# The second attention of a decoder kernel: two heads at a time on the two halves of the array's rows

## The reference

```python
qkv = x @ W_qkv + b_qkv
qkv = qkv.reshape(B, N, 3, NUM_HEADS, HEAD_DIM)
qkv = jnp.transpose(qkv, (2, 0, 3, 1, 4))
q, k, v = (qkv[0], qkv[1], qkv[2])
scores = jnp.einsum('bhqd,bhkd->bhqk', q, k) * SCALE
attn = jax.nn.softmax(scores, axis=-1)
out = jnp.einsum('bhqk,bhkd->bhqd', attn, v)
out = jnp.transpose(out, (0, 2, 1, 3)).reshape(B, N, C)
return out @ W_proj + b_proj
```

## Time and profile before

| | us |
|---|---|
| median of three runs | 2764.35 |
| profiled execution | 2767.74 |
| its span | 2765.9 |
| TensorE busy | 2511.4 (91%) |
| TensorE weight loads | 1727.1 (62%) |
| VectorE busy | 1717.4 (62%) |
| ScalarE busy | 1282.2 (46%) |
| GpSimd busy | 867.3 (31%) |

### The profile page before, as it was taken

The page is one execution under the profiler, slowest core; times in us unless marked ns, Lnnn a source line. Parts: engine busy times, 40 slices in busy tenths (PEclk is TensorE's granted clock), DMA queues, the critical chain, the costliest instruction groups (busy, mean ns, idle before and its releaser), DMA issues.

```text
span 2765.9 us, 35667 instructions
## 1 busy us (share of the span) xinstructions
PE 2511.4 (91%) x13840; PEld 1727.1 (62%) x13840; DVE 1717.4 (62%) x3089; ACT 1282.2 (46%) x2015; POOL 867.3 (31%) x445
## 2 busy tenths in 40 slices
PE   8999998999999789899999999997999999976663
PEld 7554545744554579788888988994555555544421
DVE  5566655376665446875444344356877777847967
ACT  4555554345555144344444444442666555632342
POOL 4777774366777240102222023010200000004323
PEclk9999999999999899899999999998999999987885
DMA  2000001000000210000000010003333232210000
GB/s 74 12 22 14 12 12 43 12 12 23 12 19 1 69 61 1 31 1 31 31 31 20 12 43 9 1 1 83 74 66 70 62 66 62 47 32 9 1 0 31
DMA packets 49641, 84.23 MB, mean 30 GB/s; under 512 B 9912, under 2 KB 30016, under 8 KB 49472
## 3 DMA queue, kind: packets, MB, share of 16 engines
q1 hardware_dynamic: 49328, 81.88, 11.6%
q10 hardware_dynamic: 144, 0.07, 0.0%
HBM read 37.49 MB, written 2.10 MB: 14 GB/s over the span
## 4 chain that ended last, share of the span: by engine, by line
PE 75%; DVE 16%; ACT 3%; issue 3%; POOL 2%; DMA 1%; SPq 0%; ACTq 0%; DVEq 0%; POOLq 0%
PE PS L85 74%; DVE m_gl L1097 2%; DVE PS L576 2%; DVE a_QS L554 1%; ACT a_P L519 1%; DVE a_nm L568 1%; DVE s_nm L1523 1%; DVE X L271 1%; DVE x_E L1922 1%; DVE x_rd L1906 1%; DVE st_s L232 1%; DVE x_sm L1927 1%; POOL f_H L2128 1%; POOL a_sum L676 1%; ACT a_QS L473 1%
## 5 line engine op out<-in xcount | busy, mean ns | idle before, releaser
L1097 DVE TENSOR_TENSOR m_gl<-m_g,m_gh 128x512 fp32r<-128x512 f32 x288 | 258.1, 902 | 386.4 <-ACT m_g L936 386.4
L676 POOL TENSOR_TENSOR a_sum<-a_sum,a_P 128x1024 f32<-128x1024 f32 x192 | 456.6, 2378 | 128.4 <-ACT a_P L519 118.0
L519 ACT ACTIVATE a_P<-PS 128x512 f32<-128x512 f32 x512 | 290.3, 596 | 354.3 <-PE PS L85 349.5
L933 ACT ACTIVATE m_gh<-PS,cols 128x512 fp32r<-128x512 f32 x288 | 198.5, 689 | 469.6 <-PE PS L85 469.6
L1523 DVE TENSOR_REDUCE s_nm<-PS 128x1 f32<-128x512 f32 x512 | 344.8, 688 | 70.0 <-PE PS L85 67.4
L568 DVE TENSOR_REDUCE a_nm<-PS 128x1 f32<-128x1024 f32 x256 | 300.4, 1216 | 128.2 <-PE PS L85 128.2
L85 PE MATMUL PS<-m_w2h,m_gh 128*128 128x256 f32 x1152 | 324.5, 282 | 18.9 <-DVE m_gl L1097 18.7
L1440 ACT ACTIVATE s_P<-PS 128x1024 f32<-128x1024 f32 x256 | 262.1, 1024 | 165.4 <-PE PS L85 164.8
L85 PE MATMUL PS<-m_w2l,m_gh 128*128 128x256 f32 x1152 | 323.1, 280 | 0.0
L85 PE MATMUL PS<-m_w2h,m_gl 128*128 128x256 f32 x1152 | 323.0, 280 | 0.0
L85 PE MATMUL PS<-a_P,a_V 128*64 128x512 f32 x1024 | 250.9, 612 | 0.0
(11 more groups left out here) (304 smaller groups left out, 4346.8 us busy)
## 6 DMA issues: line engine op xcount, KB each, us to landing
m_raw<-in_m_w SPq DMA_DIRECT2D x16, 1024.0 KB, 5.2
s_Q<-s_T SPq DMA_DIRECT2D x128, 128.0 KB, 2.4
s_K<-s_T SPq DMA_DIRECT2D x128, 128.0 KB, 2.4
a_KH<-a_KH SPq DMA_DIRECT2D x64, 128.0 KB, 2.3
a_wr<-in_w_qk SPq DMA_DIRECT2D x16, 256.0 KB, 2.9
X<-in_x SPq DMA_DIRECT2D x4, 512.0 KB, 6.6
a_P<-in_w_v SPq DMA_DIRECT2D x8, 256.0 KB, 5.8
a_P<-in_w_o SPq DMA_DIRECT2D x2, 1024.0 KB, 5.5
```

Of the source, the lines that this page charges most:

```text
L519: e.activation(a_P[:, g % N_P, half * 512:half * 512 + 512], PS[:, 2 + half, :], ACT.Exp).then_inc(s["a_exp"], 1)
L676: e.tensor_tensor(o[:, :], a_P[:, (g - 1) % N_P, :] if k == 1 else o[:, :], a_P[:, g % N_P, :], ALU.add).then_inc(s["a_add"], 1)
L933: e.activation(m_gh[r][:, :], PS[:, 4 + n % 3, :], func, bias=cols[:, bcol:bcol + 1]).then_inc(s["m_gh"], 1)
L1097: e.tensor_tensor(m_gl[r][:, :], m_g0[r][:, :], m_gh[r][:, :].bitcast(F32), ALU.subtract).then_inc(s["m_gl"], 1)
```

## The change

Two neighbouring heads go together as a pair (16 pairs of 16 steps, 256 steps as before). Each head's block in `Qs` and `Ks` now has 64 rows: high Q and K in 32, low Q with high K in 16, high Q with low K in 16; head a of a pair lies in rows 64a to 64a + 63 (`R[a]`). `gather(p)` issues twelve DMAs for a pair, of 32 or 16 rows, and three buffers are in use. The product of the two low parts and the low part of the maxima (`s_ml`) are left out.

In step x TensorE does: the transposed pair w = x - 13 (two products of 64 rows, one for each head, 512 queries, banks 4 and 5, now the only pair of banks for them, so it waits for the exponential of w - 1); the natural pair (two products, one for each head, 512 keys, banks 0, 1 or 2, 3 in turn); in even steps the values of two units, y - 1 and y; then the side pieces. VectorE takes the maxima of both heads in one instruction over 2 x 512 columns. `rows` still comes every eight steps, now for half of a pair's queries. The finished values are copied by ScalarE from bank 6 into `s_zt` and from there by two DMAs into `Zs`. SP has the maxima rows at x mod 8 = 1, these DMAs at x mod 8 = 6 and the gather of pair x // 16 + 2 at x mod 16 = 15, in the order of x. `values` pieces come in twos in four even steps; four of the eight `turned` are side pieces at x = 228, 236, 244 and 252.

Cut to its core (the waits renumbered for the new counts are left out):

```diff
-        R_S = 4
+        R_S = 3
...
-        s_P = [sb(c, f"s_P{i}", [128, S]) for i in range(3)]
-        nm2 = sb(c, "s_nm2", [128, 2, 8, 2])
...
-        s_mh, s_ml = sb(c, "s_mh", [8, 2, 128], FR), sb(c, "s_ml", [8, 2, 128], FR)
+        s_mh = sb(c, "s_mh", [8, 2, 128], FR)
+        s_zt = sb(c, "s_zt", [128, 2, 256])
...
+            if x >= 9 and (x - 9) % 8 == 0 and (x - 9) // 8 < 2 * N_PR:
+                side[x].append(("rows", (x - 9) // 8))
...
+            if y % 2 == 1 and 120 <= y < 128:
+                side[x] += [("values", y - 121), ("values", y - 120)]
...
+            if todo and x % 32 > 17 and x % 8 in (3, 5, 7):
                 side[x].append(todo.pop(0))
...
+            if x % 32 in (2, 6, 10, 14) and x // 32 + 1 < 8:
+                side[x].append(("proj", x // 32 + 1, (x % 32) // 4))
+            if x in (228, 236, 244, 252):
+                side[x].append(("turned", (x - 228) // 8))
...
-                    natural(x, 0)
-                extra = list(side[x])
-                if extra and extra[0][0] == "rows":
-                    piece(extra.pop(0))
                 w = x - LAG_S
-                if 0 <= w < 8 * NH:
-                    h, kt = divmod(w, 8)
-                    bk = (2, 4)[w % 2]
+                if 0 <= w < N_U:
+                    p, half, kt = w // 16, (w // 8) % 2, w % 8
                     if kt == 0:
-                        e.wait_ge(s[f"row{h % 2}"], 256 + 32 * (h // 2 + 1))
-                    if w >= 2:
-                        e.wait_ge(s["s_exp"], w - 1)
-                    for half in range(2):
-                        t = mm(e, PS[:, bk + half, :], Ks[h % R_S][:, kt * 128:(kt + 1) * 128],
-                               Qs[h % R_S][:, half * 512:half * 512 + 512], True, True)
+                        e.wait_ge(s[f"row{(w // 8) % 2}"], 256 + 32 * (w // 16 + 1))
+                    if w:
+                        e.wait_ge(s["s_exp"], w)
+                    else:
+                        e.wait_ge(s[who_old], n_old)
+                    for a in range(2):
+                        t = mm(e, PS[:, 4 + a, :], Ks[p % R_S][R[a], kt * 128:(kt + 1) * 128],
+                               Qs[p % R_S][R[a], half * 512:half * 512 + 512], True, True)
                     t.then_inc(s["s_st"], 1)
-                if x < 8 * NH:
-                    natural(x, 1)
+                if x < N_U:
+                    p, i, half = x // 16, (x // 2) % 8, x % 2
+                    if x % 16 == 0:
+                        e.wait_ge(s[f"s_g{p % R_S}"], 192 * (p // R_S + 1))
+                    if x >= 2:
+                        e.wait_ge(s["s_nr"], x - 1)
+                    else:
+                        e.wait_ge(s["s_i"], 12)
+                    for a in range(2):
+                        t = mm(e, PS[:, 2 * half + a, :], Qs[p % R_S][R[a], i * 128:(i + 1) * 128],
+                               Ks[p % R_S][R[a], half * 512:half * 512 + 512], True, True)
+                    t.then_inc(s["s_n"], 1)
                 y = x - LAG_P
-                if 0 <= y < 8 * NH:
-                    h, kt = divmod(y, 8)
-                    e.wait_ge(s["s_exp"], y + 1)
-                    if h == 16:
-                        e.wait_ge(s["s_b7"], i7["values", kt])
-                    if kt == 0 and h:
-                        e.wait_ge(s["s_za"], 2 * h)
-                        e.wait_ge(s["s_zv"], 2 * h)
-                    for q in range(4):
-                        t = mm(e, PS[32 * q:32 * q + 32, 6, 0:256], V1[:, kt, h % 16, :],
-                               s_P[y % 3][:, q * 256:q * 256 + 256], kt == 0, kt == 7)
-                    t.then_inc(s["s_pv"], 1)
-                for what in extra:
+                if y % 2 and 0 < y < N_U:
+                    for y in (y - 1, y):
+                        q, kt = y // 8, y % 8
+                        h = 2 * (y // 16)
+                        e.wait_ge(s["s_exp"], y + 1)
+                        if y // 8 == 16:
+                            e.wait_ge(s["s_b7"], n_b7["values", kt])
+                        if kt == 0 and q:
+                            e.wait_ge(s["s_za"], q)
+                        for c in range(4):
+                            part = 512 * (c % 2) + 256 * (c // 2)
+                            t = mm(e, PS[32 * c:32 * c + 32, 6, 0:256], V1[:, kt, (h + c % 2) % 16, :],
+                                   s_P[y % 4][:, part:part + 256], kt == 0, kt == 7)
+                        t.then_inc(s["s_pv"], 1)
+                for what in side[x]:
                     piece(what)
...
-                    if w >= 3:
-                        e.wait_ge(s["s_pv"], w - 2)
-                    e.activation(s_P[w % 3][:, :].rearrange("p (a n) -> p a n", a=2), PS[:, bk:bk + 2, :],
+                    if w >= 4:
+                        e.wait_ge(s["s_pv"], w - 3)
+                    e.activation(s_P[w % 4][:, :].rearrange("p (a n) -> p a n", a=2), PS[:, 4:6, :],
                                  ACT.Exp, scale=0.25).then_inc(s["s_exp"], 1)
                 y = x - LAG_P
-                if 0 <= y < 8 * NH and y % 8 == 7:
-                    h = y // 8
+                if 0 <= y < N_U and y % 8 == 7:
+                    q = y // 8
                     e.wait_ge(s["s_pv"], y + 1)
-                    for q in range(2):
-                        e.activation(Zs[h // 16][32 * (h % 4):32 * (h % 4) + 32, (h // 4) % 4, q * 256:q * 256 + 256],
-                                     PS[32 * q:32 * q + 32, 6, 0:256], ACT.Copy).then_inc(s["s_za"], 1)
-                for what in extra:
-                    if what[0] == "spread":
+                    if q >= 2:
+                        e.wait_ge(s[f"s_zd{q % 2}"], 32 * (q // 2))
+                    e.activation(s_zt[:, q % 2, :], PS[:, 6, 0:256], ACT.Copy).then_inc(s["s_za"], 1)
+                for what in side[x]:
+                    if what[0] == "rows":
...
                     slow.append(round_steps(e, own, range(6)))
-                if x < 8 * NH:
-                    natural(x, 0)
+                if x < N_U:
+                    p, i, half = x // 16, (x // 2) % 8, x % 2
+                    e.wait_ge(s["s_n"], x + 1)
+                    if x % 16 == 0 and p >= 2:
+                        e.wait_ge(s["s_red"], 2 * p - 2)
+                    e.tensor_reduce(nm2[:, p % 2, :, i, half], PS[:, 2 * half:2 * half + 2, :], AX.X, ALU.max,
+                                    negate=True).then_inc(s["s_nr"], 1)
...
-            def gather(h):
-                g, j = h // 4, h % 4
+            def gather(p):
+                g = p // 2
                 if g == 0:
                     e.wait_ge(s["s_i"], 4)
                 else:
-                    e.wait_ge(s["s_b7"], i7["proj", g, 3])
-                    e.wait_ge(s["s_st"], 8 * (h - R_S) + 8)
-                for qd in range(4):
-                    q, k = TQK[g % 2][0][qd // 2], TQK[g % 2][1][qd % 2]
-                    for o, i in ((Qs[h % R_S], q), (Ks[h % R_S], k)):
-                        e.dma_start(o[32 * qd:32 * qd + 32, :].bitcast(F32),
-                                    i[32 * j:32 * j + 32, :].bitcast(F32)).then_inc(s[f"s_g{h % 4}"], 16)
-
-            for h in range(4):
-                gather(h)
+                    e.wait_ge(s["s_b7"], n_b7["proj", g, 3])
+                if p >= R_S:
+                    e.wait_ge(s["s_st"], 16 * (p - R_S) + 16)
+                (qh, ql), (kh, kl) = TQK[g % 2]
+                for a in range(2):
+                    r, o = 32 * (2 * (p % 2) + a), 64 * a
+                    for dst, src, at_, n in ((Qs, qh, 0, 32), (Ks, kh, 0, 32), (Qs, ql, 32, 16), (Ks, kh, 32, 16),
+                                             (Qs, qh, 48, 16), (Ks, kl, 48, 16)):
+                        e.dma_start(dst[p % R_S][o + at_:o + at_ + n, :].bitcast(F32),
+                                    src[r:r + n, :].bitcast(F32)).then_inc(s[f"s_g{p % R_S}"], 16)
+
+            gather(0)
...
-                        e.dma_start(Qs[h % R_S][r:r + 1, :].bitcast(F32),
-                                    m[:, h % 2, :].bitcast(F32)).then_inc(s[f"row{h % 2}"], 16)
-                w = x - LAG_S
-                if 0 <= w < 8 * NH and w % 8 == 7 and w // 8 + R_S < NH:
-                    gather(w // 8 + R_S)
+                for what in side[x]:
+                    if what[0] == "rows":
+                        q = what[1]
+                        p, half = q // 2, q % 2
+                        e.wait_ge(s["s_mhd"], q + 1)
+                        for a in range(2):
+                            e.dma_start(Qs[p % R_S][64 * a + 16:64 * a + 17, half * 512:half * 512 + 512].bitcast(F32),
+                                        s_mh[4 * a:4 * a + 4, q % 2, :].bitcast(F32)).then_inc(s[f"row{q % 2}"], 16)
+                y = x - LAG_P
+                if 0 <= y < N_U and y % 8 == 7:
+                    q = y // 8
+                    p = q // 2
+                    e.wait_ge(s["s_za"], q + 1)
```

(25 more changed lines are left out.)

225 lines of the change are left out of this document (84 added, 141 removed).

## The result

The changed kernel takes 2790.31 us (median of 4 runs, 2783.25 to 2796.67) against 2764.29 for the kernel before beside it: a ratio of 1.0095, 95% interval 1.0068 to 1.0122. The forecast was 4 us less than before; it came out 26 us more. The profiled execution took 2792.91 us (span 2791.1, mean granted clock 0.937; before 0.955), 25.2 us above the one of before.

What follows compares the result with a forecast made beforehand. TensorE was taken to bound the old loop, then TensorE (even steps) and its loop with ScalarE (odd). Terms summed to 522.4 us against 519.6, +2.8 - 5 - 2 = -4.2: 2760 us; own range 2740 to 2775, overall 2735 to 2800.

Steps and rivals of the forecast that it cites:

- Pairs at once, steps of 1.62 and 1.68: Both products of a pair run together; odd steps 1.62 us by the ScalarE-TensorE loop, even steps 1.68 by TensorE.
- Rivals 1 and 2: Products of a pair run in turn, 2827 us, 10%; only the second strip's weights wait for the first's, 2776 us, 12%.
- Projections 1.83: 25 projections of the next heads in even steps without slack add 1.83 us each, 45.8 us.
- Pieces in odd steps 13.8: Sums, projections of Z and scalings overrun the 0.96 us TensorE slack of odd steps: 13.8 us together.
- Values 10: `values` come two in a step on one bank, the second waiting for VectorE: 4 steps, 2.5 us each.
- Turned 4.8: Four `turned` moved out of the tail into even steps, 1.05 and 0.15 behind ScalarE's copy: 4.8 us.
- The 4 carried over from the old stage: The same summing gave the old stage 507 of 519.6 us; a third of these 12.6 us is carried: 4.
- Late rows, 16 us: Every second maxima row waits behind the gather on SP; TensorE stands at x = 16k+21: 14 us even k, 2 odd.
- rival 3: The maxima rows land in time, or SP issues small DMAs faster: -20 us, 2740 us, 17%.
- The clock after these waits, 4 us: After the late-row waits the clock may drop: five times 3 to 4 us at 1.2 GHz, some 4 us.
- rival 4: TensorE, evenly half idle in the loop, loses the clock; each tenth of the loop costs 23 us: 2785 us, 11%.
- Ahead and behind: Outside the exponentials' stretch: 5 us less before the first exponential, 2 us less behind the last.

Runs made afterwards that it cites:

- the full loop: Kernel before, with a gather of twelve DMAs issued ahead of the maxima row of every second head, four of the eight DMAs cut in two: 2839.11 us, 1.0272.

## Why the prediction was wrong, point by point

- **Pairs at once, steps of 1.62 and 1.68:** right (1.61 and 1.66; 0.50 us a pair). Rivals 1 and 2 are out by the same rows.
- **Projections 1.83:** 1.74 (3.40 against 1.66). **Pieces in odd steps 13.8:** 16.0; sums 0.93 x 7 and scalings 0.14 x 12, projections of Z 0.98 x 8, not 0.8. **Values 10:** 10.8. **Turned 4.8:** 2.6. **Spread 3.6:** 2.4. **The 4 carried over from the old stage:** nothing stands there. Together 493.7 at full clock and with rows in time, where the forecast had 522.4 - 16 - 4 = 502.4: 9 too much.
- **Late rows, 16 us:** the mechanism was right, to the landing time (1.65 from the issue's start, against 1.5) and the steps x = 16k+21. The waits of even k add up to 19.1 us where 14 was forecast, those of odd k to 9.3 where it was 2; their steps are 25.1 us too long, part of that at the low clock. With the gather behind the rows the waits are gone, so rival 3 named the right remedy for what did happen.
- **The clock after these waits, 4 us:** this is the step that failed. I priced five drops of 3 to 4 us at 4 us in all; by rival 4's own price they would have been 6. There were twelve spells, up to 17 us, some 80 us of 500, and they cost 32.3 us beside what they added to the waits. The earlier trace rows showed a drop beside a stop and go stage, and I took its length from there for a loop in which TensorE is busy 0.8 of the time and not 0.98. Rival 4 had the price nearly right (each tenth of the loop at 1.2 GHz costs 23; some 0.13 of the steps were, which is 30) and gave 2785, but it named the evenly idle loop as the cause, and that alone keeps its clock at 0.99. What happened joins two things that I had as separate ones: rows late, and most late rows paid again in clock. Moving the gather behind the rows takes away both at once, 49 us; 8 us of low clock stay without any late row.
- **The sum:** 502.4 forecast without rows and clock, 493.7 measured, -8.7; rows +9.1; clock +28.3. That is 28.7 too little, and the sign follows from the last term.
- **Ahead and behind:** -7 forecast, -6.3 measured; ahead, only 2.3 of 5 came. With the gather behind the rows the first exponential starts at 1914.6, 5.1 early, and with one value batch besides at 1917.8, 1.9 early. Each is one profiled execution, with spells of low clock ahead of it in each, so these 3 us are not explained.
- The range held the time. The forecast had the sign wrong, though slower had the largest chance of the three, 0.43.
- Open: which standstill begins a spell. In the full loop twelve of fourteen of 2.7 to 4.9 us did; between 1.1 and 2.3 us, and once at 3.18, some did and some didn't, fewer where the steps around them were fuller.
- Open too, and in no theory above: the `sums`. Of the first six in the loop, four have a spell right behind them in the changed kernel, two with the gather behind the rows, three with the projections in odd steps, and none in the kernel before or with products of all 128 rows. No run moves or changes the `sums`, so that they begin a spell is not shown; that the clock can fall ahead of the standstill is.

## What to carry to other kernels

When an edit gives TensorE slack, look for what is now issued just in time: a queue that was early enough for the old order (here twelve DMAs ahead of a row of 2 KB) turns the slack into a standstill, and a standstill of a few us was paid 1.5 times (45.5 us of standing, 67.7 in the full loop) to 1.7 times (28.3 us, 49), once as waiting and once at 1.2 GHz around it. Price both in one term. And before work is batched, see which engine gets the pause: an even step that fills TensorE and an odd one that leaves it idle are no better than two middling ones, and are worse once the loop is opened or the clock falls.

## What the runs showed of the hardware

- Products that read one half of the array's rows, one after the other, ran at a granted clock of 0.64 with TensorE busy 444 of 470 us; with all 128 rows, and steps of the same length at full clock, it was 1.00 at 414 of 470. The Trainium skill (TensorE: Matmul & The Clock Gate, Part 1) has the clock follow how busy the engine is kept; the busy time in these two profiles stands the other way round, in part because products take longer at the low clock, and only the rows that a product reads were changed between them.
- The clock fell at 2140.04 us of the changed kernel, when TensorE had been busy without a pause since 2135.29; 16 products of 4 columns, one after the other, took 1.88 of these 4.7 us. In the full loop of the kernel before the same piece stands seven times without a fall behind it.
- Two products on different halves of the rows start 1 to 4 ns apart and end 0.50 us after the first starts, as one of 128 rows does; on the same half the step was 0.23 us longer for each pair.
- A row of 2 KB landed 1.65 us after the start of its issue, which took 0.6 of them; a gather's DMA took 2.3 or 2.4, counted the same way.
- Two exponentials of 512 columns back to back took 1.08 to 1.09 us, one of 1024 took 1.02.
